# Expert rows back in four loads, a last pair summed by TensorE, row lists partly made by GpSimd, and three orders changed

## The chip, the cores and the metric

One core of a Trainium2 chip runs the whole program. The metric is the device time of one execution in microseconds. Smaller is better. The engines are TensorE (PE in the rows; PEld are its weight loads), VectorE (DVE), ScalarE (ACT), GpSimd (POOL) and SyncE (SP), which here only issues DMAs.

## The reference

Eight residual stages on a stream `x` of 1024 tokens x 256, each behind a layer norm. Four are attentions (a recurrent one, a wide one with 16 heads of 128, and two grouped ones with 16 query and 4 key heads of 16), four are mixtures of experts, each with a shared expert:

```python
x = x + _L0_attn_a_ref(_layernorm(x), ...)   # stage 0
x = x + _L0_ffn_ref(_layernorm(x), ...)      # stage 1, wide shared expert (704)
x = x + _L0_attn_b_ref(_layernorm(x), ...)   # stage 2
x = x + _L0_ffn_ref(_layernorm(x), ...)      # stage 3, the same weights again
x = x + _L1_attn_a_ref(_layernorm(x), ...)   # stage 4, grouped
x = x + _L1_ffn_ref(_layernorm(x), ...)      # stage 5, narrow shared expert (176)
x = x + _L1_attn_b_ref(_layernorm(x), ...)   # stage 6
x = x + _L1_ffn_ref(_layernorm(x), ...)      # stage 7
```

Each mixture gives a token to the 2 best of 8 experts (inner width 176) by a softmax of the router's logits, computes `silu(x @ gate) * (x @ up) @ down` in them, and adds the two results by their weights to the shared expert's.

## The kernel before, in words

`ffn_stage` is called four times: with `early` true in stages 1 and 3 (the shared expert is six chunks of up to 128 inner columns, "wide") and false in stages 5 and 7 (two chunks, "narrow"). Every engine has a program of its own in program order; engines meet at semaphores only, so the order of the work is the order of the code.

Head of a stage: the norm; then the logits of the router on TensorE, copied by ScalarE and turned to rows of tokens by 128x16 products (line 473) into `token_bank`. VectorE finds the two best experts (726, 729) and `hits` (734). TensorE computes from them, in `rank` (440, 444), the place of each token in its expert's list, between the products `up(n, half)` of the shared expert: `fill` makes the gate and the up half of chunk `n` for 512 tokens, 12 products each of f32 split in high and low parts (78 to 80, the helper `product`). ScalarE makes `silu`, VectorE `h_full` (`h_of`, 701) and `h_lo` (`h_low`, 708), ScalarE `h_hi` between them; `down` multiplies chunk by chunk into the four sums `acc`, which `clear_acc` (435) zeroes first.

From the ranks VectorE makes, in 13 small steps (744 to 759), `in_slot` and `tile_hit[:, :, 2, :]`, of each of the 16 blocks of (choice, tile) which of the 23 lists (`TILES`) of 128 rows a token goes to. Lines 761 and 762 multiply it by the block's number and by the token's number in its tile; 765 makes `slot_hit` (which of 128 slots, 16 blocks of 128 columns, bfloat16) in two parts. 16 products (454, `list_rows`) turn the two into the lists, in `list_bank`, which is the same bank as `acc[0]`. Five small steps (772 to 777) give `to_row` and `from_row`, where a result row goes and an input row comes from. `rows_known` then lets GpSimd gather the rows of each list from `normed_rows` (377, eight in flight), and lets TensorE pass to the first `down`. In a wide stage TensorE does chunks 0 to 3 before the experts, in a narrow one chunk 0 up only.

`keep_busy(pe, res, bank, n)` issues `n` products of zeros (86) into an unused bank, which compute nothing.

The experts: for each list TensorE turns the rows (505), up (518), turns (529), down (542); ScalarE copies the result to `y` (665), and GpSimd scatters it to `expert_rows` (384), row `k*1024 + token`. Tail: SyncE waits for all scatters and loads the rows back into `yg` [token in tile, choice, tile, column], for each pair of tiles and each choice one load of 256 KB (358), in 1-KB runs. `add_tiles(n)` adds them by weight to `x` on VectorE (831): both choices in a wide stage, the first in a narrow one, where TensorE adds the second into `acc[n]` by a product with a diagonal of weights (594). `add_shared` (815, 819) adds `acc` to `x`; `measure` takes the next norm's statistics (117, 123).

Grouped attention, stage 4 (`causal_gqa_stage`): eight units U. TensorE's `step(U, x)`, x = 0 to 7, computes half of the scores of this unit and, for the next, of the scores whose maxima VectorE takes (`row_max`, 1876). Four pairs of banks are used in a ring; step 5 needs the pair in which the last unit's output was turned back (1695), free when VectorE has made `o_lo` from it (`low_o`, 1905), which needs ScalarE's `o_hi` (1794).

## Time and profile before

| what | us |
|---|---|
| median of 3 runs | 1657.69 |
| the runs | 1657.69, 1654.96, 1661.39 |
| the profiled execution's own time | 1660.07 |
| its span in the trace | 1658.3 |
| TensorE busy in it | 1507.7 (91%) |
| VectorE busy | 912.3 (55%) |
| ScalarE busy | 753.5 (45%) |
| GpSimd busy | 414.2 (25%) |

The mean granted TensorE clock is 0.982 of full speed. Stage 1 runs from about 418 to 554 us of the span, stage 3 from 981 to 1117, stage 4 from 1118 to 1283, stage 5 from 1283 to 1388, stage 7 from 1552 to the end. In a timeline row the first number is the start, the second the time to the end of the last of its instructions; in brackets is the idle time before it and what ended that. A product of 512 columns is listed with 0.39 us and one follows the other in 0.23, since they are pipelined.

### The profile page before, as it was taken

How to read it: one execution, taken by the hardware profiler on the slowest of the kernel's cores; microseconds unless marked ns; L12 is line 12 of the kernel's file. 1: busy time of each engine (PE TensorE's matmuls, PEld its weight loads, DVE VectorE, ACT ScalarE, POOL GpSimd, SP SyncE). 2: the span in 40 equal slices, each digit the busy share in tenths (PEclk: the TensorE clock that was granted, in tenths of full speed). 3: DMA queues.
4: the chain of work that ended last, by engine and by line, in shares of the span. 5: the costliest groups of instructions: out<-in, count | busy, mean ns of one | idle time of the engine just before them, and what ended most of it. 6: DMA issues, size and time to landing. Idle time of an engine off the chain costs nothing. (4 is left out here: it accounts for less than half of the span.)

```text
span 1658.3 us, 28587 instructions
## 1 busy us (share of the span) xinstructions
PE 1507.7 (91%) x10423; PEld 1113.4 (67%) x10452; DVE 912.3 (55%) x1972; ACT 753.5 (45%) x1872; POOL 414.2 (25%) x328
## 2 busy tenths in 40 slices
PE   6999999998899899999899979989998898999898
PEld 4778887777677667767676657766555676633566
DVE  5766666665631846555665456147654515376722
ACT  5574656563344233343334433433443443477243
POOL 2607043130235222111211012621000461100073
PEclk9999999999999999999999999998999999899999
DMA  4002010100613411000010033221000623000433
GB/s 156 27 3 88 2 65 27 52 2 1 233 53 98 149 39 37 0 21 23 13 32 1 1 107 134 86 87 47 1 2 6 218 94 107 1 1 1 176 99 124
DMA packets 43143, 99.99 MB, mean 60 GB/s; under 512 B 7184, under 2 KB 21904, under 8 KB 42896
## 3 DMA queue, kind: packets, MB, share of 16 engines
q1 hardware_dynamic: 33040, 70.05, 12.4%
q0 software_dynamic: 9984, 28.32, 5.2%
q8 instruction: 79, 1.29, 0.3%
q14 instruction: 40, 0.33, 0.1%
HBM read 80.00 MB, written 18.35 MB: 59 GB/s over the span
## 5 line engine op out<-in xcount | busy, mean ns | idle before, releaser
L871 DVE TENSOR_TENSOR s_h_e<-s_bank,s_silu_e 128x176 f32<-128x176 f32 x92 | 31.2, 341 | 181.3 <-ACT s_silu_e L653 181.3
L518 PE MATMUL s_bank<-s_expert_w,s_xe 128*128 x368 | 124.8, 462 | 1.4 <-ACT s_xe L647 0.7
L377 POOL DMA_INDIRECT s_xg<-normed_rows,s_from_row x92 | 94.0, 1022 | 111.1 <-DVE s_from_row L777 84.3
L138 POOL TENSOR_SCALAR ln_var<-ln_moments 128x4 f32<-128x4 f32 x16 | 4.0, 253 | 470.2 <-DVE ln_moments L123 274.7
L384 POOL DMA_INDIRECT expert_rows<-s_y,s_to_row x92 | 91.1, 990 | 91.6 <-ACT s_y L665 72.7
L2624 POOL TENSOR_TENSOR s_w_hi<-s_w_raw,zero 128x1024 fp32r<-128x1024 f32 x25 | 55.8, 2231 | 210.8 <-PE s_memory L80 188.0
L1232 ACT ACTIVATE s_scratch<-s_bank,s_neg_max 128x128 f32<-128x128 f32 (+3 forms) x128 | 67.2, 527 | 87.7 <-DVE s_neg_max L1322 87.7
L542 PE MATMUL s_bank<-s_expert_w,s_he 88*128 x368 | 95.9, 382 | 4.9 <-ACT s_he L659 4.9
L1322 DVE TENSOR_REDUCE s_neg_max<-s_bank 128x1 f32<-128x128 f32 (+3 forms) x128 | 59.8, 488 | 72.0 <-PE s_bank L1129 71.7
L1146 PE MATMUL s_bank<-s_probs_t,s_v 128*128 128x512 f32 (+3 forms) x256 | 76.2, 441 | 21.2 <-ACT s_probs_t L1240 21.2
L1043 POOL TENSOR_TENSOR s_w_hi<-s_w_raw,zero 128x1024 fp32r<-128x1024 f32 x11 | 23.0, 2089 | 269.7 <-PE s_bank L80 122.9
L1127 PE MATMUL s_bank<-s_k,s_q 128*128 128x128 f32 (+3 forms) x256 | 88.5, 441 | 1.5 <-DVE s_v L1317 0.8
L542 PEld LDWEIGHTS s_bank<-s_expert_w,s_he 88*128 88x128 f32 x368 | 69.2, 190 | 29.7 <-issue 6.9
L78 PE MATMUL s_bank<-xn_t_hi,s_w_hi 128*128 128x512 f32 x192 | 83.8, 436 | 3.1 <-DVE s_h_full L701 1.6
L2311 ACT ACTIVATE s_exps<-s_bank,s_rms 128x512 f32<-128x512 f32 x128 | 76.6, 695 | 20.2 <-PE s_bank L2192 20.2
L1146 PEld LDWEIGHTS s_bank<-s_probs_t,s_v 128*128 128x128 f32 x256 | 46.5, 189 | 55.7 <-ACT s_probs_t L1240 26.4
L518 PEld LDWEIGHTS s_bank<-s_expert_w,s_xe 128*128 128x128 f32 x368 | 62.7, 190 | 22.3 <-issue 2.8
L79 PE MATMUL s_bank<-xn_t_lo,s_w_hi 128*128 128x512 f32 x192 | 77.1, 402 | 0.0
L80 PE MATMUL s_bank<-xn_t_hi,s_w_lo 128*128 128x512 f32 x192 | 77.1, 401 | 0.0
L1240 ACT ACTIVATE s_probs_t<-s_bank 128x128 f32<-128x128 f32 (+3 forms) x128 | 49.0, 437 | 59.5 <-PE s_bank L1140 59.4
L1332 DVE TENSOR_SCALAR s_scratch<-s_scratch,s_row_sum 128x128 f32<-128x128 f32 (+3 forms) x128 | 68.6, 536 | 4.5
L86 PE MATMUL s_bank<-zeros 128*128 128x512 bf16 x212 | 54.5, 396 | 16.1 <-PEq L104 14.6
(398 smaller groups left out, 4321.1 us busy)
## 6 DMA issues: line engine op xcount, KB each, us to landing
s_expert_w<-in_experts SPq DMA_DIRECT2D x32, 608.0 KB, 12.7
s_w_raw<-in_wa_o SPq DMA_DIRECT2D x16, 512.0 KB, 3.5
s_yg<-expert_rows SPq DMA_DIRECT2D x32, 256.0 KB, 4.7
s_raw<-in_shared SPq DMA_DIRECT2D x16, 384.0 KB, 6.5
normed_rows<-s_ln_xn POOLq DMA_DIRECT2D x8, 512.0 KB, 10.2
s_w_raw<-in_wa_k SPq DMA_DIRECT2D x4, 512.0 KB, 4.0
s_w_raw<-in_wa_v SPq DMA_DIRECT2D x4, 512.0 KB, 3.4
s_w_raw<-in_wa_q SPq DMA_DIRECT2D x4, 512.0 KB, 4.4
```

Source lines behind the costliest of these rows:

```text
L78: pe.matmul(out, sh, mh, start=first, stop=False, skip_group_check=True)
L79: pe.matmul(out, sh, ml, start=False, stop=False, skip_group_check=True)
L80: return pe.matmul(out, sl, mh, start=False, stop=last, skip_group_check=True)
L377: pool.indirect_dma_start(out=xg[:, i % XG_RING, :], out_offset=None, in_=x_rows[:, :], in_offset=bass.IndirectOffsetOnAxis(ap=from_row[:, ...
L384: pool.indirect_dma_start(out=y_rows[:, :], out_offset=bass.IndirectOffsetOnAxis(ap=to_row[:, i:i + 1].bitcast(U32), axis=0), in_=y[:, i % ...
L518: last = pe.matmul(u_bank[i % 2][:, 0:2 * INTER], xe[:, i % 2, x], expert_of(P, i, w), start=c == 0, stop=c == DC - 1, skip_group_check=True)
L542: last = pe.matmul(y_bank[i % 2][:, 0:D], he[0:IHALF, i % 2, h], expert_of(IHALF, i, w), start=c == 0, stop=c == 1, skip_group_check=True)
L1127: pe.matmul(to, q[:, b, h * S + r * P:h * S + (r + 1) * P], k[:, b, h, 0:(r + 1) * P], start=r == UNIT_ROWS[u][0], stop=False, skip_group_ ...
L1146: last = pe.matmul(o_bank[:, j * P:S], v[:, b, j, h * DH:(h + 1) * DH], probs_t[:, j, j * P:S], start=j == 0, stop=j == TB - 1, skip_group ...
L1232: act.activation(probs[:, h % 2, r, 0:(r + 1) * P], score_bank(h, r), ACT.Exp, bias=neg_max[:, 4 * h + r:4 * h + r + 1], accum_out=row_sum ...
L1332: dve.tensor_scalar(mine, mine, one, None, ALU.mult).then_inc(probs_done, 1)
L2311: act.activation(exps[:, s % 2, g, :], s_bank[g][:], ACT.Exp, scale=rms[:, b, 1, j:j + 1]).then_inc(exp_done, 1)
```

## The change

1. In `expert_rows`, the row of a result is now `token_in_tile*16 + tile*2 + choice`, in `normed_rows` `token_in_tile*8 + tile`. So the tables and two steps of the row numbers change, the store of the normed rows and the loads of `yg` have runs of 4 KB, and the loads are four of 512 KB.
2. In a narrow stage the tail goes by pair: `add_tiles(n)`, `add_shared(n)`, `measure(n)`; and of the last pair TensorE adds both choices, with a second diagonal. In a wide stage the last chunk's `h` goes ahead of `add_tiles(1)` to `(3)`.
3. The logits are turned and ranked in two halves, in two banks. GpSimd makes the two multiples of `tile_hit`; `slot_hit` and the list products go in four parts.
4. In a wide stage `h_full(0, 1)` goes ahead of the 13 steps and both `h_lo` of chunk 0 ahead of the row numbers; the fillers around the lists go; `down(0)` begins with tiles 2 to 7, on half by half of `h_lo`, and waits for `rows_known` only before tile 0. Other counts of fillers change.
5. In the grouped attention the fillers of step 5 go, and `low_o` goes ahead of `row_max(U + 1, 1, 0)`.

```diff
@@ ffn_stage, sync @@
-            rows = y_rows[0:ROWS * P, :].rearrange("(k t p) d -> p k t d", k=TOP_K, p=P)
+            rows = y_rows[0:ROWS * P, :].rearrange("(p t k) d -> p t k d", k=TOP_K, p=P)
             for n in range(NT // 2):
-                for k in range(TOP_K):
-                    sp.dma_start(yg[:, k, 2 * n:2 * n + 2, :], rows[:, k, 2 * n:2 * n + 2, :]).then_inc(y_back[n], 16)
+                sp.dma_start(yg[:, 2 * n:2 * n + 2, :, :], rows[:, 2 * n:2 * n + 2, :, :]).then_inc(y_back[n], 16)
@@ gpsimd @@
+            pool.wait_ge(tiles_hit, 1)
+            pool.tensor_scalar(tile_hit[:, :, 1, :], tile_hit[:, :, 2, :], partition, None, ALU.mult).then_inc(hits_placed, 1)
+            pool.tensor_tensor(tile_hit[:, :, 0, :], tile_hit[:, :, 2, :], spread(block_id, TILES), ALU.mult).then_inc(hits_placed, 1)
             pool.wait_ge(x_stored, 16 * NHALF)
@@ tensor @@
-            def down(n, last_of_run):
-                pe.wait_ge(h_lo_done, 2 * n + 2)
-                for t in range(NT):
+            def down(n, last_of_run, order=range(NT)):
+                for t in order:
+                    pe.wait_ge(h_lo_done, 2 * n + t // TB + 1)
+                    if n == 0 and early and t == 0:
+                        pe.wait_ge(rows_known, 1)
+                        clear_acc(acc[0:1])
...
-                for h in range(2):
+                pe.wait_ge(hits_placed, 2)
+                for h in range(LIST_PARTS):
...
             if early:
                 up(1, 0)
-                keep_busy(pe, res, banks[1][:], 9)
                 up(1, 1)
             else:
                 keep_busy(pe, res, banks[1][:], 9)
             list_rows()
-            keep_busy(pe, res, banks[1][:], 4 if early else 14)
-            pe.wait_ge(rows_known, 1)
+            if not early:
+                keep_busy(pe, res, banks[1][:], 16)
             if early:
-                clear_acc()
-                down(0, False)
+                clear_acc(acc[1:])
+                down(0, False, (2, 3, 4, 5, 6, 7, 0, 1))
...
-            keep_busy(pe, res, up_bank[0][:], 6 if early else 0)
+            keep_busy(pe, res, up_bank[0][:], 3 if early else 0)
             down(n_shared - 1, early)
             if not early:
...
+                        if n == BY_TENSOR:
+                            pe.matmul(to, first_diagonal[:, t % 2, :], yg[:, t, 0, :], start=False, stop=False, skip_group_check=True)
+                        last = pe.matmul(to, weight_diagonal[:, t, :], yg[:, t, 1, :], start=False, stop=True, skip_group_check=True)
...
-                keep_busy(pe, res, up_bank[0][:], 11)
+                keep_busy(pe, res, up_bank[0][:], 18 if early else 11)
@@ vector @@
             if early:
                 h_of(0, 0)
+                h_of(0, 1)
...
-            dve.tensor_tensor(tile_hit[:, :, 0, :], tile_hit[:, :, 2, :], spread(block_id, TILES), ALU.mult)
-            then(dve.tensor_scalar(tile_hit[:, :, 1, :], tile_hit[:, :, 2, :], partition, None, ALU.mult))
-            for h in range(2):
+            dve.sem_inc(tiles_hit, 1)
+            for h in range(LIST_PARTS):
...
             if early:
-                h_of(0, 1)
                 h_low(0, 0)
+                h_low(0, 1)
...
+            else:
+                for n in range(NT // 2):
+                    if n < BY_TENSOR:
+                        add_tiles(n)
+                    add_shared(n, 1)
+                    if n < 2:
+                        measure(n)
@@ causal_gqa_stage, tensor @@
-                if U and x == 5:
-                    keep_busy(pe, res, held("back", U - 1)[:, 1, :], 4)
@@ causal_gqa_stage, vector @@
-                if ahead:
-                    row_max(U + 1, 1, 0)
                 if U:
                     low_o(U - 1)
                 if ahead:
+                    row_max(U + 1, 1, 0)
```

VectorE, head of stage 1, from the last step before the lists to the row numbers, before:

```order
L759 TENSOR_TENSOR s_tile_hit<-s_routing,s_in_tile 128x16x23
L761 TENSOR_TENSOR s_tile_hit<-s_tile_hit,s_routing 128x16x23
L762 TENSOR_SCALAR s_tile_hit<-s_tile_hit,s_routing 128x16x23
L765 TENSOR_TENSOR s_slot_hit<-s_slot_iota,s_in_slot 128x1024 x2
L701 TENSOR_TENSOR s_h_full<-s_bank,s_silu 128x512
L708 TENSOR_TENSOR s_h_lo<-s_h_full,s_h_hi 128x512
L772 SCALAR_TENSOR_TENSOR s_spare<-s_bank,s_routing 128x23
```

and after, where `h_full` (line 714 now) stands twice ahead of the 13 steps, shown by the first of them (761):

```order
L714 TENSOR_TENSOR s_h_full<-s_bank,s_silu 128x512 x2
L761 TENSOR_SCALAR s_full<-s_bank 128x8
...
L776 TENSOR_TENSOR s_tile_hit<-s_routing,s_in_tile 128x16x23
L781 TENSOR_TENSOR s_slot_hit<-s_slot_iota,s_in_slot 128x512 x4
L721 TENSOR_TENSOR s_h_lo<-s_h_full,s_h_hi 128x512 x2
L788 SCALAR_TENSOR_TENSOR s_spare<-s_bank,s_routing 128x23
```

Two instructions are gone from VectorE, the second `h_full` has moved up and the second `h_lo` too. TensorE at the same place, from the last product of `up(1, 1)`, before:

```order
L80 MATMUL s_bank<-xn_t_hi,s_w_lo 128x512
L454 MATMUL s_bank<-s_tile_hit,s_slot_hit 128x69 x16
L86 MATMUL s_bank<-zeros 128x512 x4
L435 MATMUL s_bank<-zeros 128x512 x4
L78 MATMUL s_bank<-s_w_hi,s_h_hi 128x256
```

and after:

```order
L82 MATMUL s_bank<-xn_t_hi,s_w_lo 128x512
L465 MATMUL s_bank<-s_tile_hit,s_slot_hit 128x69 x16
L445 MATMUL s_bank<-zeros 128x512 x3
L80 MATMUL s_bank<-s_w_hi,s_h_hi 128x256
```

The fillers are gone and three banks are cleared at once; the fourth clear follows 18 down products later. VectorE at the end of stage 7, before:

```order
L708 TENSOR_TENSOR s_h_lo<-s_h_full,s_h_hi 64x512 x2
L831 SCALAR_TENSOR_TENSOR x<-s_yg,s_token_w,x 128x256 x8
L819 TENSOR_TENSOR x<-s_bank,x 128x512 x4
```

and after:

```order
L721 TENSOR_TENSOR s_h_lo<-s_h_full,s_h_hi 64x512 x2
L845 SCALAR_TENSOR_TENSOR x<-s_yg,s_token_w,x 128x256 x2
L833 TENSOR_TENSOR x<-s_bank,x 128x512
L845 SCALAR_TENSOR_TENSOR x<-s_yg,s_token_w,x 128x256 x2
L833 TENSOR_TENSOR x<-s_bank,x 128x512
L845 SCALAR_TENSOR_TENSOR x<-s_yg,s_token_w,x 128x256 x2
L833 TENSOR_TENSOR x<-s_bank,x 128x512 x2
```

Each pair's sum follows its adds, and the last pair has a sum only.

## Rows read from the trace of the kernel before

**Rows 1.** Stretches: length, busy of each engine, granted clock, DMA share, GB/s.
```profile
430.00:449.50 19.50, 18.25 (x111) 13.20 (x111) 16.30 (x59) 6.20 (x11) 2.37 (x3) 1.00 0.69 280
...
987.40:991.00 3.60, 3.54 (x9) 2.85 (x10) 2.33 (x6) 1.38 (x3) 0.00 (x0) 0.53 0.98 297
...
530.50:533.40 2.90, 2.90 (x8) 2.30 (x7) 0.00 (x0) 0.39 (x1) 0.97 (x1) 0.50 0.16 58
1306.00:1312.00 6.00, 3.15 (x14) 1.58 (x12) 5.62 (x17) 1.45 (x5) 4.78 (x5) 1.00 0.28 84
```

**Rows 2.** Timeline of TensorE, head of stage 1.
```profile
442.50 0.50 PE L78 MATMUL s_bank<-xn_t_hi,s_w_hi 128*128 128x512 f32 x1 [0.80 <-DVE s_h_full L701]
...
444.00 0.72 PE L454 MATMUL s_bank<-s_tile_hit,s_slot_hit 128*128 128x69 bf16 x16
...
446.42 0.47 PE L78 MATMUL s_bank<-s_w_hi,s_h_hi 128*128 128x256 f32 x1
```

**Rows 3.** Timeline of VectorE, the same head.
```profile
438.10 0.54 DVE L759 TENSOR_TENSOR s_tile_hit<-s_routing,s_in_tile 128x368 bf16<-128x368 f32 x1
...
439.49 2.36 DVE L765 TENSOR_TENSOR s_slot_hit<-s_slot_iota,s_in_slot 128x1024 bf16<-128x1024 bf16 x2
...
444.76 0.18 DVE L772 SCALAR_TENSOR_TENSOR s_spare<-s_bank,s_routing 128x23 f32<-128x23 f32 x1 [1.71 <-PE s_bank L454]
...
445.50 0.18 DVE L777 TENSOR_SCALAR s_from_row<-s_to_row 128x23 int32<-128x23 int32 x1
```

**Rows 4.** Timeline of VectorE, head of stage 5.
```profile
1299.20 0.53 DVE L759 TENSOR_TENSOR s_tile_hit<-s_routing,s_in_tile 128x368 bf16<-128x368 f32 x1
...
1303.49 0.18 DVE L772 SCALAR_TENSOR_TENSOR s_spare<-s_bank,s_routing 128x23 f32<-128x23 f32 x1 [0.54 <-PE s_bank L454]
```

**Rows 5.** Timeline of VectorE and TensorE, tail of stage 5.
```profile
1383.20 0.88 DVE L831 SCALAR_TENSOR_TENSOR x<-s_yg,s_token_w,x 128x256 f32<-128x256 f32 x2 [0.51 <-DMA s_yg<-expert_rows]
1384.12 1.29 DVE L819 TENSOR_TENSOR x<-s_bank,x 128x512 f32<-128x512 f32 x2
...
1387.51 0.66 DVE L819 TENSOR_TENSOR x<-s_bank,x 128x512 f32<-128x512 f32 x1
...
1378.75 1.13 PE L594 MATMUL s_bank<-s_yg,s_weight_diagonal 128*128 128x256 f32 x4
```

**Rows 6.** Timeline of TensorE and VectorE, tail of stage 7.
```profile
1647.96 4.04 PE L594 MATMUL s_bank<-s_yg,s_weight_diagonal 128*128 128x256 f32 x16
...
1651.77 2.49 DVE L819 TENSOR_TENSOR x<-s_bank,x 128x512 f32<-128x512 f32 x4
```

**Rows 7.** Stage 4, unit 1: timelines of TensorE, VectorE, ScalarE; waits of line 1617.
```profile
1170.69 0.39 PE L1617 MATMUL s_pair<-s_q_both,s_k_hi 32*128 32x256 f32 x2 [0.50 <-DVE s_o_lo L1905]
...
1169.25 0.69 DVE L1876 TENSOR_REDUCE s_neg_max<-s_pair 128x2 f32<-128x512 f32 x1 [0.25 <-PE s_pair L1650]
1169.86 0.68 DVE L1905 TENSOR_TENSOR s_o_lo<-s_pair,s_o_hi 128x512 fp32r<-128x512 f32 x1
...
1168.31 0.60 ACT L1794 ACTIVATE s_o_hi<-s_pair 128x512 fp32r<-128x512 f32 x1
...
  DVE s_o_lo L1905: 3.0, 6
```

**Rows 8.** Groups of GpSimd by form: busy, mean ns of one, idle before.
```profile
L1536 POOL TENSOR_TENSOR s_w_lo<-s_w_raw,s_w_hi 128x256 fp32r<-128x256 f32 x4 | 2.8, 740 | 3.7 <-ACT s_w_hi L1802 3.7
L1539 POOL TENSOR_TENSOR s_w_lo<-s_w_raw,s_w_hi 128x1024 fp32r<-128x1024 f32 x1 | 2.4, 2403 | 4.7 <-ACT s_w_hi L1809 4.7
```

**Rows 9.** Timeline of GpSimd and VectorE in stage 0.
```profile
65.46 1.90 POOL L2624 TENSOR_TENSOR s_w_hi<-s_w_raw,zero 128x1024 fp32r<-128x1024 f32 x1
...
66.71 1.20 DVE L3046 TENSOR_TENSOR s_probs<-s_probs,s_row_sum 128x512 f32<-128x512 f32 x1
67.44 2.69 POOL L2627 TENSOR_TENSOR s_w_lo<-s_w_raw,s_w_hi 128x1024 fp32r<-128x1024 f32 x1
...
77.52 0.69 DVE L3046 TENSOR_TENSOR s_probs<-s_probs,s_row_sum 128x512 f32<-128x512 f32 x1
```

More of the change, by code:

```diff
@@ L36 @@
 XG_RING, Y_RING = 8, 8
+BY_TENSOR = NT // 2 - 1
+LIST_PARTS = 4
 AT_ORDER = P
@@ L431, in down, with clear_acc @@
                 last.then_inc(w_used, 1)
-            def clear_acc():
-                for bank in acc:
+            def clear_acc(some=acc):
+                for bank in some:
                     pe.matmul(bank[:], res.zeros[:, 0:P], res.zeros[:], start=True, stop=False, skip_group_check=True)
@@ L449, in list_rows @@
             def list_rows():
-                for h in range(2):
+                pe.wait_ge(hits_placed, 2)
+                for h in range(LIST_PARTS):
                     pe.wait_ge(slot_hit_done, h + 1)
-                    for j in range(h * ROWS // 2, (h + 1) * ROWS // 2):
+                    for j in range(h * ROWS // LIST_PARTS, (h + 1) * ROWS // LIST_PARTS):
                         last = pe.matmul(list_bank[:, 0:3 * TILES], slot_hit[:, j, :],
@@ L721, in _ @@
             dve.wait_ge(earlier_made, 3)
-            dve.wait_ge(logits_back, 1)
-            then(dve.tensor_copy(logits[:], token_bank[:, 0:NT * 16].rearrange("p (t g) -> p t g", g=16)[:, :, 0:GATES]))
-            for t in range(NT):
-                last = dve.max(top8[:, t, :], logits[:, t, 0:N_EXP])
-            then(last)
-            for t in range(NT):
-                last = dve.max_index(at8[:, t, :], top8[:, t, :], logits[:, t, 0:N_EXP])
-            then(last)
+            for half in range(NHALF):
+                tiles_of = range(half * TB, (half + 1) * TB)
+                dve.wait_ge(logits_back, half + 1)
+                then(dve.tensor_copy(logits[:, half * TB:(half + 1) * TB, :],
+                                     token_bank[half][:, 0:NT * 16].rearrange("p (t g) -> p t g", g=16)[:, half * TB:(half + 1) * TB, 0:GATES]))
+                for t in tiles_of:
+                    last = dve.max(top8[:, t, :], logits[:, t, 0:N_EXP])
+                then(last)
+                for t in tiles_of:
+                    last = dve.max_index(at8[:, t, :], top8[:, t, :], logits[:, t, 0:N_EXP])
+                then(last)
             then(dve.tensor_copy(at_f[:], at8[:, :, 0:TOP_K]))
@@ L772, in _ @@
             dve.scalar_tensor_tensor(spare[:], found[:, 2, :], 1.0, spare_row, ALU.subtract, ALU.mult).then_inc(spare_done, 1)
-            then(dve.tensor_scalar(row[:], found[:, 0, :], float(P), float(ROWS * P), ALU.mult, ALU.add))
-            then(dve.tensor_tensor(row[:], row[:], found[:, 1, :], ALU.add))
+            then(dve.tensor_scalar(row[:], found[:, 1, :], float(ROWS), float(ROWS * P), ALU.mult, ALU.add))
+            then(dve.tensor_tensor(row[:], row[:], found[:, 0, :], ALU.add))
             dve.wait_ge(spare_done, 1)
             then(dve.tensor_tensor(to_row[:], row[:], spare[:], ALU.subtract))
-            dve.tensor_scalar(from_row[:], to_row[:], TOK - 1, None, ALU.bitwise_and).then_inc(rows_known, 1)
-            if early:
-                h_low(0, 1)
-            else:
+            dve.tensor_scalar(from_row[:], to_row[:], TOP_K - 1, TOK - 1, ALU.logical_shift_right, ALU.bitwise_and).then_inc(rows_known, 1)
+            if not early:
                 h_of(0, 0)
@@ L810, in add_shared @@
                     dve.wait_ge(w_used, ends)
-                if ends == n_shared:
+                if ends == n_shared and (early or b < BY_TENSOR):
                     dve.wait_ge(y_added, 2 * by_vector * (b + 1))
```

58 lines of the change are left out of this document (30 added, 28 removed).

## The prediction

> **What bounds the kernel now.** I read the stretches first, then the timelines of the places that the diff touches. In the head of the first block TensorE is busy 18.25 of 19.5 us at the full clock [rows 1], and inside it the reader is to see a wait of 0.80 us for `h_full` on TensorE, only then the 16 list products at 444.00, and the first down product at 446.42, behind fillers and the clearing of the sums [rows 2]. VectorE beside it has `slot_hit` ready at 441.85 and computes the row numbers from 444.76 to 445.68 [rows 3]. So the lists wait for TensorE there, not for VectorE. After the head TensorE has no gap until the experts, so what its head saves arrives at the end of the stage. In the narrow stages (third and fourth block) nothing else is to be done: TensorE waits for the lists, then for the gathered rows, and the head is one chain through VectorE, GpSimd and a gather [rows 4]. Their tails are bound by the loads of the expert rows and VectorE's sums behind them [rows 5], in the last one by TensorE and VectorE together [rows 6]. In the grouped attention TensorE is the bound, with one hole in each of six units: fillers, and then still a wait for `o_lo` [rows 7].
>
> **Grouped attention.** Removed: four fillers in each of units 1 to 6, and the order on VectorE is turned, so `o_lo` goes ahead of one maximum. Of unit 1: VectorE is idle from 1169.00, 0.25 before its maximum, and ScalarE has `o_hi` at 1168.91 [rows 7]; so `o_lo` can run from 1169.0 to 1169.65, where it now runs 1169.86 to 1170.54 behind a maximum of 0.69. TensorE resumes at 1170.69 now; it would at about 1169.85, with the maxima behind it still in time (the moved one ends at 1170.3, and the product that needs it starts after 1170.5). Saved 0.85, six times, 5.1 us. The wait for `o_lo` has six places [rows 7]. The fillers cost nothing by themselves, since they lie inside the wait; their cover is the clock, which is taken up below. Bounds 3.0 (the recorded idle alone) and 5.4.
>
> **Head of the two wide stages.** VectorE takes the logits in two halves. The first half's work starts about 1 us earlier, but the ranking stands behind twelve products on TensorE and waited only about 0.2 for it, so 0.2 is gained. `h_full` of the second half now stands ahead of the chain: it costs its 0.6 and some wait for its product, so `tile_hit` is ready near 439.2 instead of 438.64. Then 0.85 of VectorE's work (lines 761 and 762) goes to GpSimd, and `slot_hit` is made in four parts of 0.6, 2.4 in all as now. What GpSimd needs no row shows for this size: 256 columns take 0.74 and 1024 take 2.40 [rows 8], which makes 0.98 for 368 columns and, with one operand a column, somewhat less for the other; I take 1.7 for both, bounds 1.0 and 2.2.
>
> Do the two engines overlap? A VectorE product of 128x512 from SBUF takes 0.69 alone and 1.20 when it meets GpSimd's, ending 0.55 after GpSimd's end, and GpSimd's next takes 2.69 [rows 9] where the same form alone takes 2.40 [rows 8]. They take turns. So I add: 2.4 + 1.7 = 4.1, `slot_hit` complete at 443.3 and the list at 443.55 (16 products take 0.72, and only the last part is left). That is 1.0 before the present end at 444.56, because the list no longer stands behind the wait for `h_full`. Both `h_lo` now stand ahead of the row numbers: 443.3 + 1.3 + 0.9 = 445.5 for the rows, against 445.68, no change to speak of. TensorE: three clears, then down products from 444.3; 18 of them at 0.12, the rows are known in time, one clear, six more, end near 447.4. Now the end is 446.42 + 0.30 + 23 x 0.118 = 449.4. **Saved 2.0 in each of two stages**, 4.0. Without turns the lists would be complete at 441.9, and the same working gives an end at 446.1, so 3.3 each; bound below: 0.4.
> The page "SBUF — State Buffer" of the Trainium skill (section "SBUF: two separate sides") says that a GpSimd instruction and a VectorE one with two SBUF inputs hold a common port pair in turn, for the whole instruction; `slot_hit` has two such inputs. The f32 rows agree; no row shows bfloat16. By that rule the sum is the one made here, without it the rival "no turns" below.
>
> What the removed fillers covered: TensorE would stand from 440.8 to 442.2 and nearly so to 443.5. Behind gaps on TensorE the granted clock was 0.53, little above half of 2.4 GHz, for 3.6 us at 987.4 and 0.50 at 530.5; half speed for some 3.3 us costs about 1.6. But at 1306 to 1312 TensorE was busy for 3.15 of 6 us and the clock stayed at 1.00 [rows 1]. So I count one fall in the two stages: 4.0 - 1.6 = **2.4**.
>
> **Head of the two narrow stages.** From the end of `tile_hit` (1299.73) to the list's first use (1303.49) is 3.76 now [rows 4]. After: 4.1 + 0.1 + 0.2 = 4.4, less 0.2 from the halves. **Lost 0.4 each**, 0.8. Bounds: gained 1.0 (no turns: 2.4 + 0.3, less 0.2), lost 1.9 (GpSimd second in every turn, and the clock falls before the 16 fillers). What is queued behind the new wait on GpSimd is only the gathers, which wait for the same rows anyway.
>
> **Tails of the narrow stages.** Four loads of 512 KB in 4-KB runs replace eight of 256 KB. Now VectorE waits for them four times and adds the last pair at 1383.20, then does all four sums [rows 5]; end 1388.17. After: the first pair's sum can only follow its products on TensorE at 1378.75 to 1379.88, and from there VectorE has the sums and statistics that now fill 1384.12 to 1388.17, 4.05, and two pairs of adds (2 x 0.88), so end 1385.7. The last pair goes to TensorE: four products, 2.2, done by 1385.4 even if the load is no faster, and the last sum 0.1 + 0.66 later, 1386.2. I take 1386.1. **Saved 2.1**, and the speed of the loads hardly matters. In the last stage TensorE starts the products at 1647.96 and needs 4.04 for 16 records, 5.05 for 20: end 1653.0, the last sum 1653.9 against 1654.26 [rows 6]. The earlier stores leave the last one alone in the queue; together 0.7 (0.3 to 1.2). Sum 2.8.
>
> **Nothing:** tails of the wide stages. VectorE is without a gap there and does the same work in another order; the fillers (18 for 11, 3 for 6) end where they ended, since TensorE is 1.6 earlier. The store of the normed rows in 4-KB runs is long done when the rows are asked for.
>
> **Sum.** 5.1 + 2.4 - 0.8 + 2.8 = 9.5. The profiled execution took 1660.07 (span 1658.3 and 1.8 around it), so 1650.6 on its scale; it lay 2.4 above the median of 1657.69. Forecast **1648.2**.
>
> **Rivals.** *No turns:* bfloat16 operands or the form of `slot_hit` leave GpSimd undisturbed. 5.1 + 6.6 (no idle, so no fall) + 2 x 1.0 + 2.8 = 16.5, 1641.2. For it: the row of turns is f32. Against it: both operands are read from SBUF here as there.
> *The clock falls in most heads:* both wide ones (4.0 - 3.2) and both narrow ones (a further 1.0 each): 5.1 + 0.8 - 2.8 + 2.8 = 5.9, 1651.8. For it: the two stretches at half speed [rows 1]. Against it: the one at 1306 beside them.
> *Rows farther apart:* one expert's rows now lie 8 and 16 KB apart in memory; if each gather and scatter lands 0.6 later it shows once ahead of the experts and once behind them in the narrow stages, 4 x 0.6, and the first waits of two gathers more: 9.5 - 4 = 5.5, 1652.2.
> *Slower:* the fillers in the attention held the clock. If it falls in each of the six units, at 1.6 each, that place loses 9.6 - 5.1 = 4.5; with the falls in all heads (0.8 - 2.8 + 2.8 = 0.8) the result is 3.7 slower, 1661.4. It decides from four falls in six units on. Against it: the hole that remains is about 0.5 a unit.
>
> **How the numbers follow.** Forecast 0.50, no turns 0.20, falls in the heads 0.15, rows apart 0.07, slower 0.08. The forecast's own width is 3 either way (one fall more or less, 1.6; GpSimd's time 0.5 x 4). The range takes in no turns and the falls: 1640 to 1654. More than 0.5% is 8.3 us, about what a measurement can tell: below 1649.4. Of the forecast 0.67 lies there, 0.33; with no turns 0.20 and a little of the others, 0.56 in all. Slower by that much needs the fourth rival with more than its price: 0.03.
>
> **What would show it.** In the profile after: `o_lo` ahead of the maximum, and the hole of each unit down to 0.5 without fillers. GpSimd's two instructions beside `slot_hit`: parts of 0.6 stretched to above 1 by turns show the forecast, four of 0.6 in a row the first rival. The first down product 2 us earlier after the ranking. The granted clock between the list and the down products. Sums in the narrow tails ending 3 us after the last load. I would be wrong if GpSimd took more than 1.2 for one of its two, or if the clock in the attention showed less than 1.

## The result and the profile after

The changed kernel takes 1646.38 us (median of 6 executions, 1639.45 to 1650.72) against 1657.91 of the kernel before beside it (6 executions, 1654.96 to 1662.68). The ratio is 0.993, with a 95% interval of 0.9907 to 0.9952: faster by 11.5 us, where 9.5 had been forecast. A second measurement of the same kernel gave 1641.2 against 1656.64, ratio 0.9918 (0.9892 to 0.9944).

On the page of the profiled execution (1644.44 us) TensorE is less busy by 13.2 us, and GpSimd busier by 8.7 (its two new products alone take 3.5 in each of the four heads of expert stages); these are the span and the busy time of each engine:

```profile
span 1642.7 us, 28539 instructions
PE 1494.5 (91%) x10399; PEld 1107.3 (67%) x10422; DVE 914.1 (56%) x1974; ACT 753.8 (46%) x1872; POOL 422.9 (26%) x336
```

Where the time went is best seen by stage. A stage begins with TensorE's first instruction behind the barrier. "At half" is the time in which the granted clock was at 0.50, that is 1.2 GHz, read from the stretches of the stage in slices of 1 us. Such a stretch is called a fall below. The shortest ones last 3.4 us, and one that runs over the end of a stage is counted whole in the stage in which it begins.

| stage | before, us (at half) | after | after, second profile |
|---|---|---|---|
| 0 recurrent | 418.19 (3.4) | 416.95 (0) | 417.20 (0) |
| 1 wide experts | 137.26 (10.2) | 133.30 (6.8) | 133.27 (3.4) |
| 2 wide attention | 425.80 (0) | 427.68 (0) | 425.12 (0) |
| 3 wide experts | 137.19 (10.3) | 132.16 (10.3) | 135.33 (17.1) |
| 4 grouped attention | 164.95 (10.2) | 164.10 (23.9) | 161.05 (13.6) |
| 5 narrow experts | 106.04 (3.4) | 105.78 (3.4) | 104.86 (3.4) |
| 6 grouped attention, unchanged | 162.87 (17.0) | 156.89 (0) | 157.18 (0) |
| 7 narrow experts | 106.00 (5.0) | 105.84 (4.1) | 105.79 (3.8) |

Two things stand out. Stage 6, whose code is the same, is 6 us shorter, and stage 4, where 5.1 had been forecast, only 0.9. Both follow the clock: one lost its falls, the other had more of them.

The head of stage 1 answers to [rows 1 to 3]. TensorE no longer waits for `h_full`, and has no fillers; it waits 2.15 for the lists, and it is GpSimd that ends the wait:

```profile
430.00:449.50 19.50, 17.30 (x108) 14.13 (x108) 16.95 (x41) 7.73 (x13) 7.55 (x6) 1.00 0.66 264
...
441.47 0.72 PE L465 MATMUL s_bank<-s_tile_hit,s_slot_hit 128*128 128x69 bf16 x16 [2.15 <-POOL s_tile_hit L394]
442.24 0.59 PE L445 MATMUL s_bank<-zeros 128*128 128x512 bf16 x2
442.48 0.47 PE L80 MATMUL s_bank<-s_w_hi,s_h_hi 128*128 128x256 f32 x1
```

The first row is the stretch (length, busy times, granted clock 1.00), the others are TensorE's timeline. GpSimd and VectorE beside each other there:

```profile
437.97 2.30 POOL L393 TENSOR_SCALAR s_tile_hit<-s_tile_hit,s_routing 128x368 bf16<-128x368 bf16 x1 [15.84 <-DVEq L778]
440.24 1.18 POOL L394 TENSOR_TENSOR s_tile_hit<-s_tile_hit,s_routing 128x368 bf16<-128x368 bf16 x1
...
437.95 1.29 DVE L781 TENSOR_TENSOR s_slot_hit<-s_slot_iota,s_in_slot 128x512 bf16<-128x512 bf16 x2
439.16 0.98 DVE L781 TENSOR_TENSOR s_slot_hit<-s_slot_iota,s_in_slot 128x512 bf16<-128x512 bf16 x1
440.06 0.68 DVE L781 TENSOR_TENSOR s_slot_hit<-s_slot_iota,s_in_slot 128x512 bf16<-128x512 bf16 x1
440.67 1.29 DVE L721 TENSOR_TENSOR s_h_lo<-s_h_full,s_h_hi 128x512 fp32r<-128x512 f32 x1
```

The third of VectorE's four parts takes 0.98, the others 0.68 (in [rows 3] all of `slot_hit` took 2.36), and the first `h_lo` 1.29, where two of them take 1.28 with nothing beside them (run 4 below); GpSimd's first product needs 2.30 and its second 1.18. The narrow head of stage 5, beside [rows 4]:

```profile
1290.03 0.53 DVE L776 TENSOR_TENSOR s_tile_hit<-s_routing,s_in_tile 128x368 bf16<-128x368 f32 x1
1294.98 0.18 DVE L788 SCALAR_TENSOR_TENSOR s_spare<-s_bank,s_routing 128x23 f32<-128x23 f32 x1 [1.48 <-PE s_bank L465]
```

From the end of `tile_hit` (1290.56) to the list's first use there are 4.42, against 3.76 before. The tail of stage 5, VectorE and then TensorE, beside [rows 5]:

```profile
1369.04 0.88 DVE L845 SCALAR_TENSOR_TENSOR x<-s_yg,s_token_w,x 128x256 f32<-128x256 f32 x2 [2.29 <-DMA s_yg<-expert_rows]
1371.83 0.69 DVE L833 TENSOR_TENSOR x<-s_bank,x 128x512 f32<-128x512 f32 x1 [1.92 <-PE s_bank L608]
...
1376.83 1.29 DVE L833 TENSOR_TENSOR x<-s_bank,x 128x512 f32<-128x512 f32 x2
1379.97 1.40 DVE L119 BATCH_NORM_STATS2 ln_stats<-x 128x6 f32<-128x256 f32 x4 [1.85 <-PEq L106]
...
1374.35 0.70 PE L607 MATMUL s_bank<-s_yg,s_first_diagonal 128*128 128x256 f32 x2 [0.82 <-DMA s_yg<-expert_rows]
1376.39 2.32 PE L88 MATMUL s_bank<-zeros 128*128 128x512 bf16 x10
1379.97 1.67 PE L88 MATMUL s_bank<-zeros 128*128 128x512 bf16 x7 [1.25 <-PEq L106]
```

The last sum ends at 1378.12, but VectorE then stands 1.85 before the barrier and TensorE 1.25: the barrier now waits for the 11 fillers behind TensorE's last diagonal product. In the last stage (beside [rows 6]) the last two sums start at 1637.66, end at 1639.1, and the stage at 1642.7:

```profile
1633.33 2.94 PE L608 MATMUL s_bank<-s_yg,s_weight_diagonal 128*128 128x256 f32 x12
1637.66 1.47 DVE L833 TENSOR_TENSOR x<-s_bank,x 128x512 f32<-128x512 f32 x2
```

And a unit of the grouped attention at full clock, beside [rows 7]. The product after the wait for `o_lo` comes 14.34 after that of the unit ahead:

```profile
1163.58 0.39 PE L1637 MATMUL s_pair<-s_q_both,s_k_hi 32*128 32x256 f32 x2 [0.46 <-DVE s_o_lo L1923]
...
1177.92 0.38 PE L1637 MATMUL s_pair<-s_q_both,s_k_hi 32*128 32x256 f32 x2 [0.45 <-DVE s_o_lo L1923]
...
1162.74 0.69 DVE L1923 TENSOR_TENSOR s_o_lo<-s_pair,s_o_hi 128x512 fp32r<-128x512 f32 x1
1163.35 0.68 DVE L1894 TENSOR_REDUCE s_neg_max<-s_pair 128x2 f32<-128x512 f32 x1
```

In the kernel before it was 15.25, from 1170.69 [rows 7] to this row of the next unit:

```profile
1185.94 0.38 PE L1617 MATMUL s_pair<-s_q_both,s_k_hi 32*128 32x256 f32 x2 [0.50 <-DVE s_o_lo L1905]
```

### The profile page after: what moved, and what is told of

Its sections match the earlier page's. It is cut to its first block and busy times, and to the rows that moved or that the text cites. A ratio compares the mean times of both kernels' runs of the same rounds, so it can differ in the third digit from the quotient of the medians.

```text
span 1642.7 us, 28539 instructions
## 1 busy us (share of the span) xinstructions
PE 1494.5 (91%) x10399; PEld 1107.3 (67%) x10422; DVE 914.1 (56%) x1974; ACT 753.8 (46%) x1872; POOL 422.9 (26%) x336
## 3 DMA queue, kind: packets, MB, share of 16 engines
q8 instruction: 79, 1.29, 0.3%
## 5 line engine op out<-in xcount | busy, mean ns | idle before, releaser
L1260 ACT ACTIVATE s_probs_t<-s_bank 128x128 f32<-128x128 f32 (+3 forms) x128 | 49.0, 437 | 59.5 <-PE s_bank L1160 59.4
L1894 DVE TENSOR_REDUCE s_neg_max<-s_pair 128x2 f32<-128x1024 f32 (+3 forms) x64 | 51.5, 822 | 25.7 <-PE s_pair L1668 25.0
```

## The experiments

The executions of one kernel lie 3.5 to 13 us apart, and nearly all of that goes with the clock. Over 85 executions of nine kernels (a fit with one constant for each kernel and one slope) the time rises by 9.3 us for each 0.01 that the mean granted clock is lower, and what is left over has a spread of 1.5 us. "At equal clock" below is such a constant less that of the kernel before, with its 95% interval; the changed kernel has **-11.9 +- 1.0 us** by it (12 executions against 33).

**1. The changed kernel again**, to see what of its stages repeats.

> The changed kernel again, beside the next three. Its profile had stage 4 at half clock for some 24 us against 10 before, and stage 6, whose code is unchanged, at full clock where the one before had 16 us at half. Theory 'chance': where the clock falls differs from one execution to the next, so here the stretches lie elsewhere, and stage 6 will not be 6 us shorter than before again; ratio 0.993. Theory 'caused': the same falls at the same places, stage 4 near 164.1 us and stage 6 near 156.9 us again.

Measured: ratio 0.9918 (0.9892 to 0.9944). Neither theory held as a whole. Stage 6 is at full clock again, 157.18, which chance had not foretold. Stage 4 has falls at the same two places in both profiles, 22 us into it (13.7 us at half in the first profile, 6.8 in the second) and 101; a third moved from 145 to 54. A fall in the head of stage 3, which the first profile did not have, is there: from the turn of the logits to the first turned rows of an expert it takes 41.05 instead of 39.54, so one fall in a wide head costs 1.5.

**2. The change in the attention alone.**

```diff
-                if U and x == 5:
-                    keep_busy(pe, res, held("back", U - 1)[:, 1, :], 4)
...
-                if ahead:
-                    row_max(U + 1, 1, 0)
                 if U:
                     low_o(U - 1)
                 if ahead:
+                    row_max(U + 1, 1, 0)
```

> The kernel before with the change in the grouped attention alone (no fillers in step 5, o_lo ahead of the maximum). Theory 'shape': a unit takes 14.34 us instead of 15.25 at full clock, so six units save 5.5 us: ratio 0.9967, mean granted clock as before. Theory 'the fillers held the clock': falls come in the units in most executions, mean clock below that of before, and of the 5.5 us no more than 1 is left: ratio 0.999 to 1.001.

Measured: 1647.53 us, ratio 0.9938 (0.9922 to 0.9954); at equal clock -6.3 +- 1.3. The shape pays what was worked out (5.5). Its profiled execution was the slowest of the six and had stage 4 at half clock for 20.5 us; the other five had mean clocks of 0.987 to 0.991.

**3. The changed kernel with the four fillers of step 5 back**, `o_lo` still ahead.

```diff
+                if U and x == 5:
+                    keep_busy(pe, res, held("back", U - 1)[:, 1, :], 4)
                 for_max = take("natural", V, r, p)
```

> The changed kernel with the four fillers of step 5 put back, o_lo still ahead of the maximum. Theory 'shape': four fillers need 0.85, the hole left is 0.46, so a unit takes 14.7 us, and the kernel is 2.3 us slower than the changed one: ratio 0.9945. Theory 'the fillers held the clock': stage 4 shows no falls but the one near its start, and the kernel is 2 us or more faster than the changed one: ratio below 0.992.

Measured: 1645.35 us, ratio 0.9934 (0.9916 to 0.9952), that is the time of the changed kernel. At equal clock it is 3.2 slower than the changed one (-8.7 +- 1.3); units of 14.69 had promised 2.1. What it loses there it gets back by the clock: mean 0.987 against 0.985, and stage 4, without any fall, takes 157.59. So each theory had one half. What a fall costs here can be read from the waits for `o_lo`: in the changed kernel two of them that enclose the fall at 101 us are 18.98 apart, where the same two steps take 17.49 without one (1177.92 to 1195.41). That is 1.5, in run 2 1.6, and in run 4 the falls at 53 and 101 us cost 1.6 each. The stretch 101 us into stage 4 (granted clock in the third column from the right) in the changed kernel and in this one:

```profile
1211.40:1214.40 3.00, 3.00 (x24) 1.37 (x28) 1.04 (x4) 0.69 (x2) 0.00 (x0) 0.50 0.00 0
```

```profile
1212.80:1215.80 3.00, 3.00 (x36) 2.56 (x35) 0.00 (x0) 1.20 (x2) 0.00 (x0) 1.00 0.00 0
```

**4. Both multiples of `tile_hit` on VectorE again**, all else as changed.

```diff
-            pool.tensor_scalar(tile_hit[:, :, 1, :], tile_hit[:, :, 2, :], partition, None, ALU.mult).then_inc(hits_placed, 1)
-            pool.tensor_tensor(tile_hit[:, :, 0, :], tile_hit[:, :, 2, :], spread(block_id, TILES), ALU.mult).then_inc(hits_placed, 1)
...
-            dve.sem_inc(tiles_hit, 1)
+            dve.tensor_tensor(tile_hit[:, :, 0, :], tile_hit[:, :, 2, :], spread(block_id, TILES), ALU.mult).then_inc(hits_placed, 1)
+            dve.tensor_scalar(tile_hit[:, :, 1, :], tile_hit[:, :, 2, :], partition, None, ALU.mult).then_inc(hits_placed, 1)
```

> The changed kernel with both multiples of tile_hit made by VectorE, ahead of slot_hit, as before. Theory 'GpSimd is late': the lists waited for GpSimd's second product (1.48 after slot_hit's end less the list's own time); with 0.86 on VectorE slot_hit ends at 3.25 behind tile_hit, the list 0.65 earlier than in the changed kernel in all four heads, and h_lo is not stretched: 2.6 us faster than the changed kernel, ratio 0.9915. Theory 'the split pays': the 0.86 comes on top, lists 0.4 later in each head, ratio 0.994.

Measured: 1640.99 us, ratio 0.9897 (0.9882 to 0.9912); at equal clock -15.0 +- 1.4, 3.1 better than the changed kernel. GpSimd was late. VectorE and TensorE, head of stage 1:

```profile
437.78 0.54 DVE L775 TENSOR_TENSOR s_tile_hit<-s_tile_hit,s_routing 128x368 bf16<-128x368 bf16 x1
438.24 0.32 DVE L776 TENSOR_SCALAR s_tile_hit<-s_tile_hit,s_routing 128x368 bf16<-128x368 bf16 x1
438.47 2.48 DVE L779 TENSOR_TENSOR s_slot_hit<-s_slot_iota,s_in_slot 128x512 bf16<-128x512 bf16 x4
440.88 1.28 DVE L718 TENSOR_TENSOR s_h_lo<-s_h_full,s_h_hi 128x512 fp32r<-128x512 f32 x2
...
441.01 0.31 PE L462 MATMUL s_bank<-s_tile_hit,s_slot_hit 128*128 128x69 bf16 x4 [0.29 <-DVE s_slot_hit L779]
```

The list is complete 3.58 behind `tile_hit` (the changed kernel: 4.38), `slot_hit` and `h_lo` have their own lengths, and both wide heads are 0.8 shorter (38.71 from the logits' turn to the first turned rows). In the narrow heads the list is complete 3.61 behind `tile_hit` instead of 4.42, also 0.8, and the experts end 1.2 sooner (85.80 and 85.87 into their stages instead of 87.04 and 87.01). Four heads at 0.8 make the 3.1.

**5. GpSimd's products with nothing beside them.** VectorE starts `slot_hit` behind them.

```diff
             dve.sem_inc(tiles_hit, 1)
+            dve.wait_ge(hits_placed, 2)
```

> The changed kernel, but VectorE starts slot_hit only when both of GpSimd's products are done, so that nothing of two SBUF inputs runs beside them. Theory 'turns': in the changed kernel GpSimd's first took 2.30 and its second 1.18, most of it spent waiting for VectorE's parts (its third part was stretched by 0.30, the first h_lo by 0.60); alone they take 0.3 to 0.6 and 0.6 to 0.8, 1.2 in all. Theory 'GpSimd is slow': 2.3 and 1.2 again, 3.5 in all. In both the lists come later than in the changed kernel.

Measured (one execution, 1655.3 us):

```profile
439.52 1.25 POOL L393 TENSOR_SCALAR s_tile_hit<-s_tile_hit,s_routing 128x368 bf16<-128x368 bf16 x1 [15.82 <-DVEq L778]
440.73 0.81 POOL L394 TENSOR_TENSOR s_tile_hit<-s_tile_hit,s_routing 128x368 bf16<-128x368 bf16 x1
...
441.57 2.50 DVE L782 TENSOR_TENSOR s_slot_hit<-s_slot_iota,s_in_slot 128x512 bf16<-128x512 bf16 x4 [2.22 <-POOL s_tile_hit L394]
```

Both sizes are between the two theories: 2.06 alone, 3.48 beside VectorE. So 2.06 is GpSimd's own work, and the 1.4 on top are what VectorE beside it costs (spans on GpSimd are rough in a profile, but these repeat within 0.02 in four heads of three profiles). VectorE loses only 0.9 to it. Had the two run freely, the lists would have come some 3.0 behind `tile_hit` (an estimate: 0.14 to the start, 2.50 for `slot_hit`, 0.31 for the last four products); with VectorE alone it is 3.58 (run 4), with turns 4.38. In this profile both wide heads and the narrow one of stage 5 had a fall of the clock, and both narrow tails too: in this one execution the serial order cost more than the wait that it adds to each head.

**6. The sums of the narrow tails alone**: by pair, TensorE adds both choices of the last pair, with the old eight loads and the old rows.

```diff
+                for n in range(NT // 2):
+                    if n < BY_TENSOR:
+                        add_tiles(n)
+                    add_shared(n, 1)
+                    if n < 2:
+                        measure(n)
```

> The kernel before with the sums of the narrow tails by pair and the last pair summed by TensorE, but eight loads in 1-KB runs and the old order of rows. Theory 'the order pays, not the loads': from the last expert's end to the last sum on VectorE 16.9 us in stage 5, as in the changed kernel, against 18.9 before. Theory 'the loads pay': 18 or more, since the last landing stays where it was, 4.2 us of issue behind. In both the barrier follows TensorE's 11 fillers, not VectorE, so that 0.6 of the saving does not reach the next stage.

Measured (one execution, 1649.74 us). From the end of the last expert product to the end of VectorE's last sum in stage 5: 16.89, as in all other profiles with the new order that have no fall of the clock in that tail (eight, 16.87 to 16.90), whatever the loads did: VectorE's sums start behind TensorE's first diagonal products, which begin 9.44 behind the experts here and in the changed kernel. But the barrier follows TensorE:

```profile
1378.93 1.29 DVE L823 TENSOR_TENSOR x<-s_bank,x 128x512 f32<-128x512 f32 x2
1382.82 1.40 DVE L118 BATCH_NORM_STATS2 ln_stats<-x 128x6 f32<-128x256 f32 x4 [2.60 <-PEq L105]
...
1379.26 2.32 PE L87 MATMUL s_bank<-zeros 128*128 128x512 bf16 x10
```

VectorE stands 2.60 there, 1.34 more than a barrier takes. Since the fillers follow the last landing, the loads matter after all, by way of the fillers: the next stage began 19.49 behind the experts here, 18.74 and 18.15 in the two profiles of the changed kernel.

**7. The rows' order in memory and the four loads alone.** The diff is part 1 of the change.

> The kernel before with the new order of rows in memory alone: 4-KB runs for the store and the four loads, gathers and scatters of rows that lie 8 and 16 KB apart. Theory 'no effect': from the rows' numbers to the first turned rows 3.6 to 3.9 us in the narrow heads, 61.2 us for the experts, and a tail of the old length (17.6 to 18.9 us from the experts' end to the last sum), since VectorE's sums bind it. Rival 'rows apart are slower': 0.5 us more at the first gather, and loads of yg that start over 0.5 later behind the last scatter.

Measured (one execution, 1651.63 us). In stage 5 the next stage began 18.51 behind the experts' end (20.14 in the profile before, 18.85 in run 2), the last sum ended 17.25 behind (18.88, 17.59). VectorE adds each pair as it lands, and then has all four sums:

```profile
1378.05 0.88 DVE L831 SCALAR_TENSOR_TENSOR x<-s_yg,s_token_w,x 128x256 f32<-128x256 f32 x2 [0.33 <-DMA s_yg<-expert_rows]
...
1382.35 0.66 DVE L819 TENSOR_TENSOR x<-s_bank,x 128x512 f32<-128x512 f32 x1
```

So the loads by themselves bring some 0.3 to 1.6 in the old order. The new order brings 0.7 to 2.0 of VectorE's time with the old loads (18.88 and 17.59 to 16.89) and 0.4 with the new ones (17.25 to 16.89); the two do not add, both cut at the same wait. The start of the loads, behind the last scatter, lies 3.3 to 4.5 after the experts in either layout (5.5 once, in run 5 with a fall there) and spreads as much as the effect. From the row numbers to the first turned rows it takes 4.09 and 3.78 (before 3.63 and 3.73; with either layout elsewhere 3.70 to 4.06), and the experts are no longer. Over all profiles this stretch is on average 0.2 longer in stage 5 with the new layout (ten profiles against three), and under 0.1 in stage 7. So the rival of the rows apart costs at most 0.4, once.

**8. Two fillers instead of four in step 5**, on run 4: they just fit the hole.

```diff
+                    keep_busy(pe, res, held("back", U - 1)[:, 1, :], 2)
```

> The kernel with the multiples on VectorE, and two fillers in step 5 of the grouped attention (0.42 us, where the hole before o_lo is 0.46). Theory 'fillers hold the clock': a unit takes 14.34 to 14.40 us and stage 4 has fewer falls (none at +53 and +101 us, where all four profiles without fillers have one at +101), some 157 to 158 us; about 2 us faster than without them. Theory 'chance': stage 4 has falls as before, 161 us, and the time is the same, ratio 0.990.

Measured: 1637.79 us, ratio 0.9904 (0.9878 to 0.993), mean clock 0.9880. Units of 14.34, as without fillers, and no fall 53 or 101 us into stage 4. But two falls at 22 and 141 us kept the stage at 160.25, so the 2 us are not shown: the means of run 4 and of this one, 1640.1 and 1638.5, differ by less than they spread. They were also measured on two chips, on which the medians of the kernel before differ as much, 1656.64 and 1655.04. The filler's place in a unit, where each row is one wait or filler of TensorE (of the two fillers the trace holds one, since some records are missing):

```profile
1157.90 0.39 PE L1662 MATMUL s_pair<-s_k_hi,s_q_both 32*128 32x256 f32 x2 [0.44 <-ACT s_exps L1800]
1158.79 0.38 PE L88 MATMUL s_pair<-zeros 128*128 128x512 bf16 x1
...
1172.24 0.39 PE L1662 MATMUL s_pair<-s_k_hi,s_q_both 32*128 32x256 f32 x2 [0.45 <-ACT s_exps L1800]
```

**9. One multiple by ScalarE**, on run 8.

```diff
+                    if n == (1 if early else 0):
+                        act.wait_ge(tiles_hit, 1)
+                        act.activation(tile_hit[:, :, 1, :], tile_hit[:, :, 2, :], ACT.Copy, scale=partition).then_inc(hits_placed, 1)
...
-            dve.tensor_scalar(tile_hit[:, :, 1, :], tile_hit[:, :, 2, :], partition, None, ALU.mult).then_inc(hits_placed, 1)
```

> The kernel before this one, with the multiple by the token's number made by ScalarE instead of VectorE. ScalarE is idle there from 438.56 in the head of stage 1 and in the whole head of stage 5. Theory 'the head is VectorE's chain': slot_hit starts 0.23 to 0.30 earlier in each of the four heads and is not stretched by ScalarE; 1.0 us in all, ratio 0.0006 lower than without. Theory 'ScalarE disturbs or comes late': slot_hit is stretched as beside GpSimd, or the list waits for ScalarE in the wide heads; no gain.

Measured: 1639.13 us, ratio 0.9905 (0.988 to 0.993).

```profile
438.43 0.61 ACT L644 ACTIVATE s_tile_hit<-s_tile_hit,s_routing 128x368 bf16<-128x368 bf16 x1
...
437.91 0.54 DVE L779 TENSOR_TENSOR s_tile_hit<-s_tile_hit,s_routing 128x368 bf16<-128x368 bf16 x1
438.37 2.49 DVE L782 TENSOR_TENSOR s_slot_hit<-s_slot_iota,s_in_slot 128x512 bf16<-128x512 bf16 x4
```

ScalarE disturbs nothing (2.49), but `slot_hit` starts only 0.12 earlier behind `tile_hit` (0.61 for 0.73), since the signal to ScalarE ahead of the other multiple delays that by 0.11 on VectorE. 0.1 a head can't be seen in the time.

**10. Four fillers on run 4.**

> The changed kernel with the multiples on VectorE and all four fillers back in step 5 of the grouped attention. Stage 4 took 157.6 us without a fall in the one profile with o_lo moved and four fillers, and 161.0 to 164.1 with a fall at +101 us in all five profiles without fillers. Theory 'fillers hold the clock': stage 4 near 158 us, units of 14.69 us, no fall at +53 and +101; as fast as with two fillers or without, or faster: 1637 to 1640. Theory 'chance': stage 4 has falls again and the longer units cost 2 us against none: 1642.

Measured: 1640.29 us, ratio 0.9902 (0.9882 to 0.9922), mean clock 0.9878; stage 4 took 161.25 with falls at 22 and 145 us. At equal clock 2.4 slower than run 4, and the same in time. So the 157.59 of run 3, one profile, is not what four fillers give each time.

**11. Seven fillers instead of 11 at the end of stage 5**, on run 4.

```diff
-                keep_busy(pe, res, up_bank[0][:], 18 if early else 11)
+                keep_busy(pe, res, up_bank[0][:], 18 if early else 7)
```

> The kernel with the multiples on VectorE and 7 instead of 11 fillers at the end of the narrow stage 5. In six profiles with the new tail the next stage began 3.6 to 3.7 us after TensorE's last diagonal product, and 1.26 after VectorE's last sum only where the loads landed early. Theory 'the fillers bind': the next stage begins 18.15 us after the experts' end whatever the loads do, 0 to 0.8 us sooner. Rival 'they hold the clock': a longer gap on TensorE before the barrier, and the clock falls at the start of stage 6, as it did in the kernel before; stage 6 grows by 1 us.

Measured: 1642.1 us, ratio 0.9906 (0.9886 to 0.9926), no gain in time over run 4. The fillers bound, by 0.2: VectorE now waits only for the barrier itself, and the next stage begins 18.17 behind the experts, in run 4 18.41. No fall came at the start of stage 6.

```profile
1375.28 1.40 DVE L119 BATCH_NORM_STATS2 ln_stats<-x 128x6 f32<-128x256 f32 x4 [1.28 <-PEq L106]
```

The best of the versions tried are those with the multiples off GpSimd, runs 4 and 8 to 11, at 1637.8 to 1642.1, 0.990 to 0.991 of the kernel before. By their times the measurements can't choose among them; at equal clock run 10, with four fillers, is behind run 4.

## Why the prediction held, point by point

**Grouped attention.** Forecast 0.85 a unit, measured 0.91, so 5.5 for 5.1. The hole that remains is 0.46, as foretold. This is the largest term, and its mechanism held. The rival of the falls is half true. In the six profiles without fillers in step 5 (both of the changed kernel, runs 2, 4, 5, 11) the clock fell 101 us into stage 4 each time; in the seven with two or four of them it never did (before, and runs 3, 6 to 10). In four of the six a second one came at 53 us, in none of the seven. The price of a fall there was rightly put at 1.6 (run 3: 1.5 to 1.6); the number was not six but one or two, so without fillers the stage gives back 1.5 to 3 of the 5.5. The profiles with fillers have other falls (141 to 149 us into the stage in five of the seven), and over the whole program a fall of 3.4 us goes with 1.0 only, by the slope (3.4 us at half take 1.7 of 1650, or 0.00103, from the mean clock). Among the versions with the new order the mean clock is 0.9858 without those fillers (29 executions) and 0.9874 with two or four (23), worth 1.5 us, but the difference, 0.0016 +- 0.0018, is not clear of noise; and the kernel before, which has them too, is at 0.9853 (33). So that the fillers hold the clock at that one place is shown, that they raise it over the kernel is not. "It decides from four falls in six units on" was never reached.

**Head of the wide stages.** Forecast 2.0 saved in each, measured 2.27 from the logits' turn to the experts, and 0.2 ahead of it. The change of order behind this is what was foretold: TensorE no longer waits for `h_full` ahead of the lists. The lists came 4.38 behind `tile_hit`, and 4.35 had been worked out. That agreement is partly luck and hides two errors. GpSimd's work was 2.06, not 1.7. And the turns are not the full ones that the sum was made with: 2.4 + 2.06 would be 4.5 for `slot_hit` itself, but `slot_hit` was complete 2.9 behind `tile_hit`, and it was GpSimd's second product that came last, at 3.6. What ended TensorE's wait was thus another than foretold; the forecast had `slot_hit` complete at 4.1 and only the last products behind it, in fact `tile_hit` was complete at 3.6 and all 16 products, 0.72, behind it. The sign that I had named for being wrong, "more than 1.2 for one of its two", came true (2.30, and 1.25 alone), yet no head came out worse for it than foretold; the price shows beside what run 4 reaches. Of the two signs for the mechanism, parts of `slot_hit` stretched to above 1 stood for turns and four of 0.6 for none: one part took 0.98 and three 0.68, so the rows lie between them. And "the clock in the attention less than 1", the other sign of being wrong, came true as well (23.9 and 13.6 us at half in stage 4, 10.2 before), with the time met all the same. The first down product came 25.53 into stage 1 instead of 28.23, 2.7 earlier where 2 had been named.

The page "SBUF — State Buffer" of the Trainium skill (section "SBUF: two separate sides") has the loser blocked for the whole instruction of the other. Here VectorE's products were stretched by 0.30 (bfloat16) and 0.60 (f32), while GpSimd's own work was 2.06: the contention is there for bfloat16 too, the full hold on VectorE is not what these rows show.

**The clock in the heads.** One fall was counted in the two wide stages, 1.6. The first profile has none, the second has one, at 1.5. Both wide heads of run 5 have one, and none of runs 3, 4 and 8 to 11. (In the narrow heads, about 25 us into the stage, runs 6, 8 and 9 have one in both and run 10 in one; the two profiles of the changed kernel have none.) So one fall in two stages was counted too dear: over the two profiles of the changed kernel it is one in four heads.

**Head of the narrow stages.** Forecast 0.4 lost in each. From the turn of the logits to the first turned rows it was 17.10 and 17.20 before, 17.81 and 17.53 after; over three profiles with the old heads (before, runs 2 and 6) and three with the changed ones (both of the changed kernel, run 3) the means are 17.17 and 17.59, so 0.42 lost, as forecast. The parts are: the list came 4.42 behind `tile_hit`, as worked out (4.4, from 3.76), 0.66 later; the halves gained 0.4 and not 0.2 (`tile_hit` ends 8.80 and 8.81 behind the turn before, 8.42 and 8.40 after); the first gathered rows came 0.4 and 0.1 later. In this one profile the experts ended 1.1 and 0.8 later in their stages. What goes beyond the head is 0.4 from the start of stage 5 to the turn (7.95 for 7.54; it spreads from 7.4 to 8.0 over all kernels) and 0.3 in the length of the experts in stage 7 (61.50 for 61.18), a part that had been put at nothing. In the three profiles with the changed heads the experts of the narrow stages take 61.3 to 61.7, with the old heads and no fall 61.2 to 61.3; why stays open. GpSimd itself costs 0.8 in each list (run 4): over the four profiles with both multiples on VectorE the turn to the first rows takes 16.73, so that without GpSimd the part would have gained 0.4.

**Tails of the narrow stages.** Forecast 2.1 in stage 5 and 0.7 in stage 7. VectorE's last sum came 16.89 behind the experts, from 18.88: 2.0. The forecast had put it at 1386.1, and 16.89 behind the experts of that profile is 1386.18, so this path was worked out rightly. The 18.88 is not the same each time: the loads began 4.50 behind the experts in that profile and 3.26 in run 2, with 17.59. Of the 2.0 only 1.4 reached the next stage (2.0 in the second profile), since TensorE's 11 fillers were the new bound, a wait that the forecast had not looked at (run 11). Stage 7 gained 0.9. Sum 2.3 for 2.8. "The speed of the loads hardly matters" holds for VectorE (run 6), not for the barrier.

**Wide tails: nothing**, and 0.1 longer in fact (23.34 for 23.24 from the experts' end to the next stage, where no fall came in it).

**Sum.** 5.5 + 2 x (2.27 + 0.2 - 0.1) - 1.9 + 2.3 = 10.6 from the two profiles at full clock, against 11.1 in the forecast before its 1.6 for the clock, and 11.9 +- 1.0 by the executions at equal clock; the 1.9 are the two profiles' own, and with 0.42 for each narrow head it is 11.7. The 1.6 counted for the clock did not come as a net cost: the mean clock is 0.9853 before (33 executions) and 0.9850 after (12). So the forecast of 9.5 lies below the 11.5 measured mainly by that term. The profiles themselves lie 15.6 apart; the rest is the clock, 59.5 us at half before and 48.5 after, worth some 3 by the slope, and the spread. Stage 6, which nobody touched, had 17.0, 0 and 0 us at half in the three profiles above, and 0 to 13.7 in the other kernels. What decides that stays open; neither the changed tail ahead of it nor the fillers in stage 4 sort the profiles cleanly.

**The rivals.** No turns (1641.2) falls: run 5 has GpSimd's products at 2.06 without VectorE and 3.48 with it. That a median came out at its number (1641.2 in the second measurement) is no sign of it. Falls in most heads: one of eight in the two profiles, in a wide one. Rows apart: at most 0.4 at the first gather. Slower: one or two falls in the units instead of six, and the time is lower.

## What to carry to other kernels

Before work is given to an idle engine, time it there beside what runs at that moment. 0.86 us of VectorE's work became 3.5 on GpSimd, 1.4 of it only because VectorE worked beside it, and doing it where it was is 3 us faster over the kernel. When the end of a stage is pulled in on one engine, look at what the others have queued ahead of the barrier: fillers that once fitted under a longer tail become the bound. A filler that fits into a hole costs nothing; one that is longer than the hole costs its excess in each pass, and here the clock gave back about as much and no more (run 3).

## What the runs showed of the hardware

Most of the spread between executions of one program goes with TensorE's granted clock: 9.3 us for each 0.01 of its mean, with 1.5 us left over. A profile should therefore be compared by stages that have the same time at half clock, and a difference of a stage in unchanged code (6 us here) is no effect of the change. The falls of 3.4 to 13.7 us came where TensorE had just had gaps, often at the same places of the program (22 us into stage 4 in 11 of 13 profiles, where TensorE waits 1.0 and then 0.7 to 1.3 for VectorE's maxima). Runs 3 and 6 have the same waits there and no fall, so the gaps alone do not decide it. A fall of 3.4 us under TensorE's products cost 1.1 to 1.4 in the wide tail (24.35 for 23.24 before, 24.74 for 23.34 in the second profile after), 1.5 in the wide head and 1.5 to 1.6 in the grouped attention.

A GpSimd product of 128x368 in bfloat16 takes 1.25 with one factor for each partition and 0.81 for two tensors, where VectorE needs 0.32 and 0.54: on GpSimd the form with one tensor is the longer one, on VectorE the shorter.
